# Cross attention and experts on one core: K's and Q's stacks as a ring of three chunks, probabilities of four key tiles, one run of value products per quad

## The reference

```
n1 = _ln(x, ln1_g, ln1_b)
q = jnp.einsum('btd,mdhk->mbhtk', n1, mha_wq) + mha_bq[:, None, :, None, :]
kk = jnp.einsum('btd,mdhk->mbhtk', n1, mha_wk) + mha_bk[:, None, :, None, :]
v = jnp.einsum('btd,mdhk->mbhtk', n1, mha_wv) + mha_bv[:, None, :, None, :]
scores = jnp.einsum('mbhtk,mbhsk->mbhts', q, kk) / jnp.sqrt(jnp.float32(KD))
attn = jax.nn.softmax(scores, axis=-1)
ctx = jnp.einsum('mbhts,mbhsk->mbthk', attn, v)
```

## Time and profile before

| | us |
|---|---|
| median of 2 runs | 1390.99 |
| lowest, highest | 1388.59, 1393.39 |
| the profiled execution | 1391.66 |
| its span, first to last instruction | 1390.0 |
| PE / DVE / ACT / POOL busy | 1334.1 / 1086.8 / 893.2 / 372.0 |
| granted TensorE clock over the span | 0.989 |

### The profile page before, as it was taken

One profiled execution on the slowest core, in us unless ns is written; L12 is line 12 of the kernel. 1 busy time (PEld: TensorE's weight loads), 2 busy tenths in 40 slices (PEclk: granted clock), 3 DMA queues, 4 the chain that ended last, 5 costly groups with the idle time before them and its releaser, 6 DMA issues.

```text
span 1390.0 us, 23079 instructions
## 1 busy us (share of the span) xinstructions
PE 1334.1 (96%) x7542; PEld 658.4 (47%) x7666; DVE 1086.8 (78%) x2371; ACT 893.2 (64%) x1696; POOL 372.0 (27%) x371
## 2 busy tenths in 40 slices
PE   7988989999999999999999999999999999999989
PEld 5733424455444554445444554445444454443356
DVE  7768997988779787888779887797869887787731
ACT  3256667685677657776577756876567765757751
POOL 7521243224213051122312152130512223122000
PEclk8899999999999999999999999999999999999999
DMA  4012102211222103212132112222031211212002
GB/s 119 17 37 87 47 31 96 85 44 54 78 83 78 62 25 106 77 65 73 36 110 82 43 54 83 79 78 69 26 121 54 84 55 44 76 36 91 17 0 91
DMA packets 96656, 90.23 MB, mean 65 GB/s; under 512 B 20832, under 2 KB 91616, under 8 KB 95644
## 3 DMA queue, kind: packets, MB, share of 16 engines
q1 hardware_dynamic: 96540, 88.75, 19.4%
HBM read 35.05 MB, written 4.25 MB: 28 GB/s over the span
## 4 chain that ended last, share of the span: by engine, by line
PE 32%; issue 8%; DVE 6%; SPq 2%; ACT 1%; POOL 1%; DMA 0%; DVEq 0%; another core or an unknown queue 0%; ACTq 0%; POOLq 0%
PE psum L903 5%; PE psum L918 5%; PE psum L872 4%; PE psum L853 4%; DVE mx L1426 4%; PE psum L888 4%; PE psum L735 2%; PE psum L497 2%; SPq L2038 2%; PE psum L770 1%; PE psum L520 1%; ACT prob L1746 1%; PE psum L608 1%; PE psum L581 0%; DVE resid L1297 0%
## 5 line engine op out<-in xcount | busy, mean ns | idle before, releaser
L1746 ACT ACTIVATE prob<-psum 128x512 f32<-128x512 f32 x1024 | 553.7, 603 | 295.6 <-PE psum L918 209.2
L1426 DVE TENSOR_REDUCE mx<-psum 128x1 f32<-128x512 f32 x1024 | 640.3, 681 | 58.6 <-PE psum L888 56.4
L903 PE MATMUL psum<-qst,kst 128*128 128x512 bf16 x902 | 270.8, 382 | 18.0 <-issue 9.4
L918 PE MATMUL psum<-prob,vst 128*17 128x512 f32 x2048 | 246.4, 595 | 1.4 <-ACT prob L1746 1.1
L888 PE MATMUL psum<-kst,qst 64*128 64x512 bf16 x1024 | 176.7, 383 | 16.3 <-DVE resid L1297 5.4
L888 PEld LDWEIGHTS psum<-kst,qst 64*128 64x128 bf16 x1024 | 48.6, 93 | 206.6 <-issue 171.4
L903 PEld LDWEIGHTS psum<-qst,kst 128*128 128x128 bf16 x1024 | 82.1, 98 | 131.3 <-issue 76.8
L872 PE MATMUL psum<-w,cxT 128*128 128x256 f32 x448 | 106.4, 384 | 0.0
L1896 POOL CAST parts<-resid 128x512 bf16<-128x512 f32 x64 | 39.7, 620 | 248.2 <-DVE resid L1297 248.2
L918 PEld LDWEIGHTS psum<-prob,vst 128*17 128x17 f32 x2048 | 45.8, 96 | 122.3 <-issue 97.8
L853 PE MATMUL psum<-n2T,x 128*128 128x512 f32 x224 | 102.5, 597 | 0.0
(11 more groups left out here) (250 smaller groups left out, 1716.2 us busy)
## 6 DMA issues: line engine op xcount, KB each, us to landing
kst<-parts SPq DMA_DIRECT2D x372, 64.0 KB, 2.0
qst<-parts SPq DMA_DIRECT2D x372, 64.0 KB, 2.0
cmat<-G_dram SPq DMA_DIRECT2D x7, 1024.0 KB, 4.6
x<-in_L_ffn_fw SPq DMA_DIRECT2D x14, 512.0 KB, 3.3
w<-in_L_ffn_fw SPq DMA_DIRECT2D x14, 512.0 KB, 4.2
xbuf<-in_x SPq DMA_DIRECT2D x8, 512.0 KB, 4.6
kin<-in_ctx SPq DMA_DIRECT2D x8, 512.0 KB, 3.7
out<-acc SPq DMA_DIRECT2D x7, 512.0 KB, 3.0
```

What stands on the lines that cost most here:

```text
L903: e.matmul(psum[:, u.bank, :], kst[:, par, h // 2, g * P:(g + 1) * P], qst[:, par, h // 2, :], start=True, stop=True).then_inc(u.full, 1)
L918: ins = e.matmul(psum[32 * j:32 * j + VW, VB, :], vst[:, g, h, :], prob[:, g % 2, j, :], start=g == 0, stop=g == NT - 1, tile_position=(0, ...
L1426: e.tensor_reduce(mx[:, qq, par, j, t:t + 1], psum[:, u.bank, :], AX, ALU.max).then_inc(u.free, 1)
L1746: e.activation(prob[:, g % 2, j, :], psum[:, u.bank, :], ACT.Exp).then_inc(u.free, 1)
```

## The change

The stacks keep three chunks of heads, not four: 12 tiles instead of 16, and a chunk overwrites the one three before it (`tile`). `stack` waits for the last score of that old chunk. The room goes to `prob`, which holds four key tiles. The exponent of tile g waits for the products of tile g in the quad before. All four tiles' value products of a quad are one run, at slot 0 of the next quad: 64 runs. The copy of the context moves from slot 3 to slot 4 (`COPY`). The memsets and the DMA of ones cover 8 tiles, not 12. All lists are new; of the lists, the diff below keeps AHEAD, MIDDLE's lists of SP and the second half's of PE.

```diff
-        kst = sb("kst", [P, 2, M * H // 2, S], BF16)
-        qst = sb("qst", [P, 2, M * H // 2, S], BF16)
+        RING = 3
+        kst = sb("kst", [P, 2, RING * HP, S], BF16)
+        qst = sb("qst", [P, 2, RING * HP, S], BF16)
...
-        prob = sb("prob", [P, 2, QUAD, S])
+        prob = sb("prob", [P, NT, QUAD, S])
...
-        VALUES, COPY, TURN = 0, 3, 7
+        VALUES, COPY, TURN = 0, 4, 7
...
         FIRST = dict(
-            AHEAD="3103010200000310100120002002010211010011120000000100000012000200"
-                  "0000010400000010010110101100301010000000010100020002010010000000")
+            AHEAD="3014003100000020200101001030010301101010001101000200000002000002"
+                  "0000000101100110101201001201000120000000010110002010100100000000")
         MIDDLE = dict(
-            PE_S=slots(5, "p4 p5:16 p6:0 p7:16 v0:15 v1"),
+            PE_S=slots(5, "p4 p5:17 p6:0 p7:13 v0:16 v1"),
-            SP_A=slots(1, "ctx:2 x:11 gi:7 G:71 s0 s1:14 s2:10 s3"),
-            SP_C=slots(57, "w10:2 w20:10 w11:2 w21:36 out"),
-            SP_S=slots(11, "s4:9 s5:4 s6:39 s7"),
-            AHEAD="2101000102001112020000201000100021010001200010000000000022020002"
-                  "0200010022002100210100002201000210000000200101100101000010000000")
+            SP_A=slots(1, "ctx x:6 gi:9 G:67 s0:11 s1:10 s2:12 s3"),
+            SP_C=slots(41, "w10:13 w20:4 w11:15 w21:45 out"),
+            SP_S=slots(4, "s4:11 s5:23 s6:14 s7"),
+            AHEAD="2102001000100201200200200100000120020101000200000000010002020202"
+                  "1200000002002200210101000021020020000100010010012100010000000000")
         LAST = dict(
-            AHEAD="2100210000011112210120001002000022000000000101011001010000020020"
-                  "2200020022000200201101002001000020101000000010000010001100000001")
+            AHEAD="2101020100002002220021000012000203000100001000000000001000102222"
+                  "2201000002000200201011000001010023000001004000000000000000000000")
...
+        def tile(b, h):
+
+            return (b * M * KC + h // HC) % RING * HP + h % HC // 2
...
-                    ins = e.matmul(psum[32 * j:32 * j + VW, VB, :], vst[:, g, h, :], prob[:, g % 2, j, :], start=g == 0,
+                    ins = e.matmul(psum[32 * j:32 * j + VW, VB, :], vst[:, g, h, :], prob[:, g, j, :], start=g == 0,
...
-                            if (b > 0 or slot >= 2 * QUAD) and slot % (2 * QUAD) == VALUES:
-                                for n in (slot // QUAD // 2 * 2 - 2, slot // QUAD // 2 * 2 - 1):
-                                    values(*divmod(b * NQ + n // NT, NQ), n % NT)
+                            if b + qq > 0 and slot % TILES == VALUES:
+                                for n in range(NT):
+                                    values(*divmod(b * NQ + qq - 1, NQ), n)
...
-                    values(B - 1, NQ - 1, NT - 2)
-                    values(B - 1, NQ - 1, NT - 1)
+                    for n in range(NT):
+                        values(B - 1, NQ - 1, n)
...
-                if j == 0 and n > 1:
-                    e.wait_ge(valued, n - 1)
-                e.activation(prob[:, g % 2, j, :], psum[:, u.bank, :], ACT.Exp).then_inc(u.free, 1)
+                if j == 0 and n >= NT:
+                    e.wait_ge(valued, n - NT + 1)
+                e.activation(prob[:, g, j, :], psum[:, u.bank, :], ACT.Exp).then_inc(u.free, 1)
...
-                if b > 0:
-                    w = uses["score", b - 1, NQ // M * (m + 1) - 1, NT - 1, QUAD - 1]
+                old = b * M * KC + m * KC + c - RING
+                if old >= 0:
+                    w = uses["score", old // (M * KC), NQ // (M * KC) * (old % (M * KC) + 1) - 1, NT - 1, QUAD - 1]
                     e.wait_ge(w.full, w.n)
-                p0 = (m * H + c * HC) // 2
+                p0 = tile(b, m * H + c * HC)
```

More of the change, by code:

```diff
@@ new lines, in build @@
+            DVE_S=slots(5, "s4:4 s5:14 s6:7 s7"),
+            ACT_A=slots(2, "kT0:7 kT1:0 qT0:0 qT1:3 gpart grow1:0 grow0:2 fa:16 mask00:0 mask01:0 mask02:0 mask03:0 "
+                           "mask10:0 mask11 mask12:0 mask13 mask20:2 mask21 mask22:2 mask23:0 mask30:4 mask31:2 "
+                           "mask32:2 mask33:0 decexp:17 sq0 sq1:18 n1T0:0 n1T1 p0:7 p1:3 p2:8 p3:2 pv0:23 pv1 logits"),
+            ACT_C=slots(-1, "cxT00:14 cxT01:0 cxT10:2 cxT11:25 n2T0:3 n2T1:5 logits:11 hid00 hid01 hid02:0 hid03:13 "
+                            "hid10 hid11:0 hid12:0 hid13"),
@@ new lines, in build @@
+            ACT_S=slots(5, "p4:2 p5:15 p6 p7:14 v0:16 v1"),
+            POOL_A=slots(3, "pw:11 vcopy:17 mask0:17 mask1:15 mask2:4 mask3:0 vw hw:0 hs:0 hn:5 x2:7 r1:0 r5:3 s0:0 "
+                            "s1:3 s2:2 s3"),
+            POOL_C=slots(30, "acc0:0 r1"),
+            POOL_S=slots(15, "s4:15 s5:15 s6:3 s7"),
+            SP_A=slots(1, "ctx x:6 gi:9 G:67 s0:11 s1:10 s2:12 s3"),
+            SP_C=slots(41, "w10:13 w20:4 w11:15 w21:45 out"),
+            SP_S=slots(4, "s4:11 s5:23 s6:14 s7"),
@@ L385, in build @@
-            ACT_S=slots(5, "p4 p5:14 p6:3 p7:6 v0:10 v1"),
+            ACT_C=slots(1, "cxT00:3 cxT01:7 cxT10:0 cxT11:34 n2T0:0 n2T1:6 logits:10 hid00:0 hid01:2 hid02:0 hid03:16 "
+                           "hid10:52 hid11:0 hid12:0 hid13"),
+            ACT_S=slots(7, "p4:4 p5:10 p6:2 p7:6 v0:7 v1"),
             POOL_A={},
-            POOL_C=slots(14, "acc0:36 r1"),
-            POOL_S=slots(-1, "s4:0 s5:0 s6:29 s7"),
+            POOL_C=slots(43, "acc0:5 r1"),
+            POOL_S=slots(12, "s4:6 s5:19 s6:0 s7"),
@@ L389, in build @@
             SP_A={},
-            SP_C=slots(48, "w10:2 w20:20 w11:61 w21:4 out"),
-            SP_S=slots(-1, "s4:19 s5:18 s6:26 s7"),
-            AHEAD="2100210000011112210120001002000022000000000101011001010000020020"
-                  "2200020022000200201101002001000020101000000010000010001100000001")
+            SP_C=slots(46, "w10:8 w20:10 w11:69 w21:2 out"),
+            SP_S=slots(-1, "s4:16 s5:15 s6:8 s7"),
+            AHEAD="2101020100002002220021000012000203000100001000000000001000102222"
+                  "2201000002000200201011000001010023000001004000000000000000000000")
@@ L887, in maximum @@
                     own = HALVES[par]
-                    e.matmul(psum[:, u.bank, :], qst[own, par, h // 2, t * P:(t + 1) * P],
-                             kst[own, par, h // 2, :], start=True, stop=True).then_inc(u.full, 1)
+                    e.matmul(psum[:, u.bank, :], qst[own, par, tile(b, h), t * P:(t + 1) * P],
+                             kst[own, par, tile(b, h), :], start=True, stop=True).then_inc(u.full, 1)
             def max_rows(b, qq):
@@ L901, in score @@
                     u = take("score", b, qq, g, j + par)
-                    h = qq * QUAD + j + par
-                    e.matmul(psum[:, u.bank, :], kst[:, par, h // 2, g * P:(g + 1) * P], qst[:, par, h // 2, :], start=True,
+                    h = tile(b, qq * QUAD + j)
+                    e.matmul(psum[:, u.bank, :], kst[:, par, h, g * P:(g + 1) * P], qst[:, par, h, :], start=True,
                              stop=True).then_inc(u.full, 1)
```

77 lines of the change are left out of this document (33 added, 44 removed), and 12 rows, old and new, of the table DVE_A.

## The result

| | before | after |
|---|---|---|
| median of 2 runs | 1390.99 | 1405.44 |
| lowest, highest | 1388.59, 1393.39 | 1403.66, 1407.22 |
| span of the profiled execution | 1390.0 | 1402.0 |
| granted TensorE clock over the span | 0.989 | 0.994 |

The ratio of after to before is 1.0109 (95% interval 1.0085 to 1.0133). I had forecast 1382 us in a range from 1370 to 1395. The sign was wrong and the range missed.

A forecast was written before the change was run, and what follows sets the result against it. TensorE, 96% busy, was taken to bound the kernel. The terms -10.8 - 1 + 1 + 1 + 2 - 0.9 gave -8.7 us, from 1391.7 to 1383; with the median 0.7 lower, 1382 us, range 1370 to 1395.

The forecast's parts named there:

- Array changes: PE's value runs: 128 become 64, array changes fall from 790 to 710, exits are saved; -10.8 us, bounds 8 and 14.
- Bunching: DVE runs dry about half a microsecond a quad beside the 3.56 us run; +1 us, bounds 0 and +8.
- No gain: bunching: Rival: DVE runs dry during the products, then holds PE's banks; 1392 us, chance 0.18.
- Four tiles of probabilities: ACT loses roughly half its 209.2 us wait, PE gets score banks sooner; -1 us, bounds 0 and -6.
- The copy one exponent later: ACT's context copy moves from slot 3 to 4, transposes stay at slot 7; +1 us, bounds 0 and +6.
- The ring: SP's chunk loads: every list position lies behind the release, no wait is reached early; cost nothing.
- the start: DVE's memsets shrink from 2.62 to 1.75 us, one directly before a scan; -0.9 us, bounds -0.9 and -2.6.
- SP at the border: SP's queue between periods makes PE wait 0.6 us at each of seven borders; +2 us, bounds 0 and +10.
- the tail: All four tiles' products come behind the last score, where two did; nothing, bounds -1 and +1.
- The slower rival: SP's queue takes over at the period borders, PE waiting 2.5 us at each; 1398 us, chance 0.17.

The follow-up runs named there:

- both engines light: DVE's row maximum over 128 of 512 keys, ACT's exponent over 256 of 512 queries: 1365.8 us on the kernel before, 1364.3 on the changed one.
- the ring alone: The kernel before with only the ring of three chunks and the smaller memsets: 1388.9 us, ratio 0.9997.
- two runs: Changed kernel's ring and four probability tiles, two value runs a quad, lists of before: 1385.9 us with copy at slot 4, 1381.3 at slot 3.
- each small move of mine: Changed kernel with run cut in two: 1448.8 us; all transposes of maxima one slot later: 1492.6; only last quad's, two slots later: 1405.3; copy at slot 3: 1404.2.
- a mismatch: Changed kernel in the lists of before: 1487.5 us; also with maxima over a quarter of the keys and exponents over half the queries: 1400.7 us.
- 16 waits of 51.7 us: Changed kernel with the transposes of the row maxima one slot later everywhere, SP's send in its old slot: 1492.6 us, ratio 1.0743.

## Why the prediction was wrong, point by point

- **Array changes, -10.8 us.** There are 64 runs of x32, each 3.56 us to the next start (709.29 to 712.85), a pass is still 0.43 and the exit 0.12, as forecast. To price the term I took each gap between two groups of PE's instructions, less the shortest usual gap of its kind (the 15th percentile, worked out from both traces of a pair). What is left for work is 152.3 us a middle period before and 151.6 after with both engines light, 152.6 and 152.0 with full work; in the first period it falls by 3.0 to 3.2. My count has 8 changes less in a middle period, 0.8 us, plus the exits. That makes about 7 us over the first seven periods, with the last not measured. It is an estimate that depends on how the gaps are sorted: other sortings of the same traces give 0.2 to 0.8 us for a middle period, one of them 3.7, and 1.1 to 5.2 for the first. So some saving is likely, its size is not shown, and it was not what decided. In the changes of both traces it is 0.09 to 0.12 us for each, so the 175 ns of the Trainium skill ("TensorE: Matmul & The Clock Gate", Single matmul latency) are not seen here either.
- **Bunching, +1 us, bounds 0 and +8.** This is the step that failed. I named a mechanism and set its point: "From 0.14 us a quad more than I took, the whole 8.7 us is eaten." PE's waits behind DVE's maxima alone grew by 14.8 us, 0.23 us a quad; those behind ACT did not grow (8.6 and 8.8 us). I priced it by how long DVE runs dry beside the run and asked whether DVE could catch up over a quad. Its own wait did not grow. But PE does not wait for an average: the last maxima of a quad, their copy and their transposes are a chain, and where a second run used to cover it nothing does now. I had no term for that. The rival "No gain: bunching" (1392) had PE held behind DVE, with its price too small and its place only half right: 10.0 of the 24.1 us stand within 4 us of a long run's end. (The 3.8 us a quad that I gave DVE as free are 3.6 by the earlier trace rows.)
- **Four tiles of probabilities, -1 us, bounds 0 and -6.** ACT's wait fell from 209.2 to 97.1 us, as forecast. Beside the ring alone, in the lists of before, the four tiles gave 7.6 us. The value lay beyond my bound of 6, and the bound was worked out wrongly: half of the 3.4 us per 200 that PE idles is about 12 us over the span, so the same words give 24. I had read that PE hardly waits behind ACT and taken that for the worth of the change. With one run the four tiles were not measured by themselves.
- **The copy one exponent later, +1 us, bounds 0 and +6.** 4.6 us with two runs, nothing to be measured with one.
- **The ring, 0, and the start, -0.9.** Ring and start together: -1.0 us by the medians (interval of the ratio 0.9983 to 1.0010). The memset is 1.76 us, and the scan behind it starts at 22.99 instead of 24.51:

```profile
21.29 1.76 DVE L1035 MEMSET qst<- 64x2048 uint32 x1 [0.38 <-issue]
22.99 1.15 DVE L1038 TENSOR_TENSOR_SCAN cmat<-onecol,cmat 4x512 f32<-4x512 f32 x1
...
26.31 2.08 PE L700 MATMUL psum<-mid,ident 128*128 128x512 f32 x2 [4.11 <-DVE mid L1046]
```

  PE's product comes 1.53 us earlier than in the earlier trace rows, more than the one memset's 0.86. The memset itself starts 0.67 us earlier (21.29 against 21.96); I take it that an earlier one stands on the chain too. The other 2.2 of the start's 3.7 us are no more than a start varies by: in twelve traces with the small memsets and full work the first score starts between 89.5 and 92.4 us, in two with the large ones at 92.5 and 94.3. My bounds held.
- **SP at the border, +2, and the tail, 0.** SP's four stacks start at 682.47, 691.79, 701.37 and 709.04 us, and the last send is issued by 718.71, 2.4 us ahead of the period's first score at 721.1; in the earlier trace rows it was 1.5. The changed kernel's waits list none of PE for the rows' DMA. The slower rival was wrong in its place: PE is late there before SP is.

```profile
717.27 1.44 SPq L2101 DMA_DIRECT2D qst<-mrow  x2
```

Put together by the medians: ring -1.0, four tiles -7.6, later copy +4.6, and the long run with its lists +19.6, against my -8 or so for the same (array changes, bunching, border). The four add up to 15.6, the case's 14.5 and the scatter of a median.

What stays open: whether some other lists would let the long run win. The change came with lists of its own, and each small move of mine from them was neutral or cost 43 to 87 us, so no kernel here shows the best that one run can do. How the 19.6 us divide between lost cover, an engine that runs dry and the other places of the new lists is not shown: no pair of kernels with the same fitting lists differs in the run alone. The 36 us of a mismatch that light engines leave are not explained either.

## What to carry to other kernels

When PE is the bound and other engines have slack, merging its instructions into a longer run has a price that no busy share shows: a run no longer stands where it covered another engine's latency, and that engine may also run dry beside the longer one. Price it at each chain that a run used to cover (last product, the other engine's copy, the next use on PE), start to start, rather than by whether the other engine can catch up over a period. And undo a change in parts that keep lists and runs matched: here that found the parts worth having (1381.3 us), which the whole had hidden.

## What was unexpected of the hardware

- The stalls of about 4 us cost more than themselves here: with 16 waits of 51.7 us in all behind the rows' DMA the kernel took 87 us more. PE stood 4.33 us until 687.5, and from 688.6 to 691 us the granted clock was 0.50, the lower of its two levels (1.2 GHz); a value run took 5.48 us instead of 3.56; over 500 to 700 us it was 0.95 against 1.00 in the changed kernel.
- ACT loads its function tables 86 times with the new lists and 62 with those of before, whatever the runs and the ring, 1283 ns each. That is 30.8 us more work for ACT, whose busy time grew by 27.1. At the exponents' line it is 40 times instead of 28. Whether any of it reaches PE was not tested; PE's waits behind ACT are 8.8 and 8.6 us. The Trainium skill ("ScalarE: Activation LUTs", What ACT_TABLE_LOAD costs) states the same 1283 ns for the load.

```profile
L1752 ACT ACT_TABLE_LOAD x40 | 51.3, 1283 | 16.7 <-PE psum L924 16.1
```

- A value run's exit costs about 0.12 us: 0.54 us pass from the start of a run's last pass to the next start, against 0.43 for a pass, in all 30 runs of the changed kernel with a maximum behind and in 20 of 26 of the kernel before with a score behind (the other six show 0.77, as if the record of one score, 0.22, were missing). A little over half of the runs of the kernel before with a maximum behind took 0.62; why is open.
